# Ranking each group of four graphs by itself in the second graph layer

## What is computed

```python
x = x + gnn0(layernorm(x), adj)     # softmax(leaky_relu(s1+s2) masked by adj) @ h, then elu
x = x + ffn0(layernorm(x))          # 8 experts, the best two of each row, weighted
x = x + gnn1(layernorm(x), adj)     # the same attention with other slopes, then relu
x = x + ffn1(layernorm(x))          # 32 experts of width 32
# ffn1:
logits = xf @ router_w.T + router_b
idx = argmax(logits)                # one expert for each of the 16384 rows
h = relu(xf @ W1[idx] + b1[idx])
out = relu(h @ W2[idx] + b2[idx])
```

## Time and profile before

| | us |
|---|---|
| median of 3 executions | 1198.93 (1197.79 to 1203.39) |
| profiled execution, its own time | 1197.08 |
| its span | 1195.3 |
| PE busy over the span | 948.1 (79%) |
| DVE busy | 791.0 (66%) |
| POOL busy | 781.6 (65%) |
| ACT busy | 708.2 (59%) |

### The profile page before, as it was taken

How to read it: one execution, slowest core, us unless ns; L and a number is a source line. 1 busy time by engine, 2 the same in 40 slices (tenths; PEclk the granted TensorE clock), 3 DMA queues, 4 the chain that set the end, 5 groups by cost and what they waited for, 6 DMA issues and landing times. The chain is left out here.

```text
span 1195.3 us, 27365 instructions
## 1 busy us (share of the span) xinstructions
PE 948.1 (79%) x6789; PEld 839.2 (70%) x6789; DVE 791.0 (66%) x3492; ACT 708.2 (59%) x2414; POOL 781.6 (65%) x989
## 2 busy tenths in 40 slices
PE   5888988887179999999994899999960667666873
PEld 4677877776079999999994688888850555544653
DVE  6688898889459999999994378888873121121221
ACT  3998898886035656555552899999930333322431
POOL 4357777777617787877776048778785366666666
PEclk9999897987579999999997999999975655666555
DMA  9133432211367777777772113232213442223210
GB/s 207 37 120 118 139 102 61 60 51 38 95 180 207 203 205 206 208 203 207 196 203 60 36 51 87 76 86 76 60 42 109 109 111 83 74 82 85 64 35 8
DMA packets 147913, 130.88 MB, mean 109 GB/s; under 512 B 26450, under 2 KB 119484, under 8 KB 147760
## 3 DMA queue, kind: packets, MB, share of 16 engines
q1 hardware_dynamic: 125456, 93.02, 30.4%
q0 software_dynamic: 18272, 34.21, 8.4%
q10 hardware_dynamic: 4032, 1.89, 0.5%
HBM read 83.28 MB, written 49.61 MB: 111 GB/s over the span
## 5 line engine op out<-in xcount | busy, mean ns | idle before, releaser
L477 POOL DMA_INDIRECT xs<-staged,dst x256 | 258.9, 1011 | 77.6 <-issue 68.5
L1067 ACT ACTIVATE hT<-bank,wt 128x128 f32<-128x128 f32 x620 | 177.2, 369 | 133.4 <-PE bank L1274 81.4
L528 POOL DMA_INDIRECT out<-oq,xq x160 | 159.9, 999 | 112.2 <-DVE oq L978 66.3
L506 POOL DMA_INDIRECT x2d<-ob,xi x155 | 163.6, 1055 | 43.3 <-issue 29.1
L1260 PE MATMUL bank<-xnT,wt 128*128 128x128 f32 x1240 | 166.9, 278 | 0.7 <-issue 0.4
L1274 PE MATMUL bank<-w2s,hT 128*128 x1240 | 165.5, 276 | 0.7 <-DVE ob L951 0.5
L978 DVE SCALAR_TENSOR_TENSOR oq<-bank,xq 128x512 f32<-128x512 f32 x40 | 27.7, 692 | 197.1 <-remote 103.2
L1260 PEld LDWEIGHTS bank<-xnT,wt 128*128 128x128 f32 x1240 | 152.6, 194 | 3.1 <-issue 2.5
L1274 PEld LDWEIGHTS bank<-w2s,hT 128*128 128x128 f32 x1240 | 150.9, 192 | 1.8 <-issue 1.2
L1101 ACT ACTIVATE xnqT<-bank 128x512 f32<-128x512 f32 x40 | 23.9, 596 | 164.0 <-remote 71.0
L1016 ACT ACTIVATE p<-bank,nm 128x128 f32<-128x128 f32 x256 | 103.1, 403 | 19.1 <-DVE nm L699 13.9
(11 more groups left out here) (202 smaller groups left out, 2313.9 us busy)
## 6 DMA issues: line engine op xcount, KB each, us to landing
wt<-wpd SPq DMA_DIRECT2D x155, 258.0 KB
xq<-xs SPq DMA_DIRECT2D x160, 66.0 KB
xi<-xs SPq DMA_DIRECT2D x155, 66.0 KB
xb<-x2d SPq DMA_DIRECT2D x32, 258.0 KB
xb<-in_x SPq DMA_DIRECT2D x32, 256.0 KB
wpd<-w1c SPq DMA_DIRECT2D x56, 129.0 KB
xs<-staged,dst POOLq DMA_INDIRECT x256
out<-oq,xq POOLq DMA_INDIRECT x160
```

The source lines that it names most:

```text
L477: pool.indirect_dma_start(out=xs[l], out_offset=bass.IndirectOffsetOnAxis(ap=dst[b % ND][:, c:c + 1], axis=0), in_=stag[s][:, q, 0:ROW], i ...
L506: pool.indirect_dma_start(out=x2d, out_offset=bass.IndirectOffsetOnAxis(ap=xi[t % NXI][:, ID:ID + 1].bitcast(U32), axis=0), in_=ob[:, t % ...
L528: pool.indirect_dma_start(out=orow, out_offset=bass.IndirectOffsetOnAxis(ap=xq[j % NXQ][:, q, ID:ID + 1].bitcast(U32), axis=0), in_=oq[j % ...
L1067: last = act.activation(hT[t % 2][:, j, :], HID[t % 2][:, j, :], ACT.Gelu, bias=wt[t % NW][:, c:c + 1])
```

## The change

In layer 1 the table now holds 32 batches of one group in place of 16 batches of two; layer 0 keeps its pairs.

```diff
-BATCH = [[(2 * b, 2) for b in range(NG // 2)] for l in range(2)]
+BATCH = [[(2 * b, 2) for b in range(NG // 2)], [(g, 1) for g in range(NG)]]
```

## The result

The changed kernel took 1206.16 us (median of 11 executions, 1203.84 to 1209.66), the kernel before 1200.61 us (11, 1197.79 to 1204.42): ratio 1.0046, 95% interval 1.0034 to 1.0059. It is slower by 5.5 us (interval 4.1 to 7.1), where +3.8 was forecast. The profiled execution took 1206.29 us with a span of 1204.5, 9.2 us over that of before.

The account below looks back on a forecast made before the run. The prediction took layer 1's odd steps to be a latency loop through `route1` and `nm`; 0.15 + 7.92 - 0.53 + 0.64 - 5.07 + 0.7 = +3.8 us gave 1202.7 us, own range 1199.5 to 1206, 8 in 10 range 1196 to 1207.5.

Parts of the forecast that it names:

- Two of the signs that I had named for being wrong: Layer 1: a step under 7.0 or over 7.25 us; quick fills not beginning 2.4 us behind the last scatter.
- first rival: Layer 1 steps: the narrow loop is shorter and POOL's own work sets the pace, 1189.6 us; chance 0.07.
- the second (6.81 stays): Layer 1 steps: the pace stays at 6.81 us because slack before `pm` hides something counted, 1194.0 us; chance 0.10.
- The price of a narrow operation: DVE, layer 1: a linked operation of 128 columns takes 0.31 us, 0.01 either way, so a step is 7.14 us.
- fourth rival: PE's rank product before every transpose of `staged` adds a wait above 0.1 us per step, over +6 us; chance 0.12.
- The start of the fills: End of layer 1: last power +8.2 us, with a shorter chain behind it, so fills begin +6.1 us later, at 909.7.
- The tail, -5.07: POOL, end of layer 1: six groups of scatters in place of seven, each leaving a step sooner, saves 5.07 us.
- fixed time behind the last scatter: End of layer 1: fills crawl while scatters are under way, quick ones begin 2.4 us behind the last scatter.
- third rival: End of layer 1: fills take as long as before whatever POOL does, the late `filli` decides, 1205.0 us; chance 0.13.
- Pace: Layer 1, steps 8 to 31: 24 steps of 7.14 us in place of 6.81, +7.92 us.
- start: Layer 1, steps 6 and 7: a narrow `route1` added in step 6 moves the first `pm` of step 8 by +0.15 us.
- fills: End of layer 1: 1.4 fewer fills done in the crawl come after it at 0.52 us each, +0.7 us.

Follow-up runs that it names:

- e1: Changed kernel with `places` moved behind `scores` in layer 1 (second `oh` buffer); ratio 1.0018 to the kernel before.
- e2: Changed kernel with `scores` (`nmax`, `nm`) put ahead of `route1` in layer 1; ratio 1.0021 to the kernel before.
- e10: Changed kernel with one more, repeated linked operation of 128 columns in `route1` of layer 1; ratio 1.0172 to the kernel before.
- e6: Changed kernel, unaltered, run again on another occasion; 1149.93 us, ratio 1.0077 to the kernel before.
- e4: Changed kernel, but in layer 1 SP and ACT wait for all scatters before issuing the fills; ratio 1.0149 to the kernel before.
- e12: Changed kernel with layer 1's fills issued only after all scatters, run on a further occasion; ratio 1.0154 to the kernel before.
- e3: Changed kernel, but each group of layer 1 leaves one step later on POOL, as before; ratio 1.0075 to the kernel before.
- e11: Changed kernel with each group of layer 1 leaving one step later on POOL, run on a further occasion; ratio 1.0093 to the kernel before.
- e9: Kernel before with 15 pairs and two single groups in layer 1, the last power ahead of one group's scatters; ratio 1.0003 to the kernel before.
- e5: Kernel before, with pairs, but in layer 1 DVE does the scores ahead of `route1`; ratio 0.9993 to the kernel before.
- e8: Kernel before, with pairs, but POOL does the last three powers of layer 1 ahead of the scatters; ratio 0.9988 to the kernel before.

## Why the prediction was right in the main, and where it was off

The direction and the size held: +5.5 us was measured for +3.8, and the ratio of 1.0046 lies inside the 0.5% that had a chance of 0.67. The time of 1206.16 lies inside the range for 8 in 10 (1196 to 1207.5) but just over my forecast's own range (1199.5 to 1206). 1.7 us of the miss in time is the median of before, 1200.61 in 11 executions for 1198.93 in three. Two of the signs that I had named for being wrong did show: the mean step is 7.31 us with an ordinary one of 7.25, and the quick fills began 2.1 us behind the last scatter and not 2.4.

**What bounds a step: right.** Singles removed the alternation, each step is the loop of latencies from `pm` to `pm`, ACT and POOL wait as told. e1 and e2 take a part out of the loop, and the step falls until DVE is full; e10 puts one in, and it grows by just that part. The first rival (POOL's pace) and the second (6.81 stays) are excluded by the 7.25.

**The price of a narrow operation: too low.** "I take 0.31 and give it 0.01 either way." The seven links of a step (five in `route1`, two in `places`; I had counted nine) take about 0.325 us each; `route1` is 1.83 in place of 1.76 and `places` 0.92 in place of 0.88. A step is 7.25, just over the 7.23 that I had allowed: +2.6 us in 24 steps. The 0.31 was the interval from `lgb` to its waiter, the one narrow row that I used. It is still 0.31 in the changed kernel (792.34 to 792.65), but `lgb` is the quick one: it lasts 0.28, the others of this width 0.29. The wide ones (0.457 for a duration of 0.42, so 0.037 between end and start) and the 0.29 of `pm`, which has the same width, would have given 0.29 + 0.037 = 0.327. The Trainium skill's 75 ns per instruction (Vector Engine (DVE) Microarchitecture Reference, 5.2 Measured stream behaviour on trn2) was still further off for linked operations, as the prediction assumed.

**A term that I didn't have: PE's clock.** Singles leave PE idle for about 1 us in every step where before it was nearly full (114.28 of 120 us, now 104.98). In one step of this profile the clock was low, for 1.24 us. Together with 2.6 this explains 3.9 of the 4.1 us by which the 24 steps missed. The drop belongs to the execution and not to the kernel alone: e6 has none in these steps. By its size (12.01 / 24 = 0.50 us more in each step in place of 0.33) the pace is the fourth rival's, above 0.1 us over mine, but not by its mechanism: no wait for the rank product showed.

**The start of the fills: too early.** I had put it 6.1 us later, at 909.7; it was 914.05, 10.4 later, or 11.4 counted from the first `nm` of the layer. 4.2 of the 5.3 us between are the pace and the start; the rest was not taken apart. By the account above it cost nothing here, since the last scatter decided.

**The tail, -5.07 and the fixed time behind the last scatter: held at this level, not at the other.** In the pair of profiles the tail is -4.56 (forecast -4.96), and the first `xnq` follows the last scatter by 14.2 to 15.6 us in all four kernels profiled at the 1200 us level, although their fills start 8.4 to 15.9 us ahead of it. At the 1141 us level this time runs from 7.0 to 12.7 us (e4 and e12 apart, whose fills wait), and the profiles of e3 and e11 put the sooner leave at 0.5 to 1.6 us there. So at that level the start of the fills counts, which the change delays by more than 10 us, and the third rival's idea comes nearer. The change's price points the same way, ratio 1.0077 there (8.6 us) against 1.0046 (5.5 us), but the two intervals overlap. At the 1200 us level e9 shows that a sooner start of the fills gains nothing; e3 wasn't measured there, so that the -5.07 is real is argued from the profiles, not shown by undoing it. That the forecast was made from, and measured at, the level where its rule for the tail holds is luck: the prediction did not know of the other.

**The sum.** Pace +4.1, start +0.1, tail +0.4, fills -1.0, end -0.03 make the +3.8 into the +7.4 us of the layer. The medians differ by 5.5. The 1.8 us between the two is within what the two profiled executions differ from their medians (0.1 and 3.5 us); it was not taken apart further.

## What to carry to other kernels

Splitting a batch halves the width of its operations but not their price: from 256 to 128 columns a linked operation went from 0.457 to 0.325 us. Ask first which steps had slack: here pairs put the two chains in different steps, one of which hid its chain under another engine's work, and singles paid both in each step. Take the interval of linked operations as duration plus the gap seen between linked ones of any width, and multiply by the number of links times steps; about 0.015 us for each became 2.6. Before a term rests on how a tail ends, look for what else could end it, and whether that holds in another execution.

## What the runs showed of the hardware

The same program has two levels on different occasions, 1141 to 1143 and 1199 to 1203 us, and the chip that gave 1141 us for e5 to e8 gave 1202 us for e9 and e10; no comparison here crosses them except where said. The pace of graph layer 1 is equal at both (changed kernel: 7.25 us a step), so the difference lies elsewhere. Of the 55.0 us between the changed kernel's span and that of e6, the same kernel, 9.1 lie ahead of the layer's first `nm`, 3.0 from there to the first `xnq`, and 42.9 in mixture 1. Of the 3.0 the step with the low clock has 1.1, and the stretch behind the last scatter the other 2.0. The second level shows itself in SP's 16 fills: 8.94 us (e6) against 15.72 (changed). In such a crawl not only the transfers are slow: the view of line 316 in the kernel before has SP's register moves from 905 to 919 us at a median of 686 ns, and those from 919.5 to 924 us at 29. The views by line from 940 to 1130 us, for the kernel before at the 1200 us level and then for e6:

```profile
L528 POOL DMA_INDIRECT out<-oq,xq x119 | 119.2, 1002 | 94.3 <-DVE oq L978 59.7 <-issue 34.5
L1304 PE MATMUL bank<-xnqT,vq 128*32 128x128 f32 x250 | 54.6, 392 | 39.6 <-issue 39.6
```

```profile
L528 POOL DMA_INDIRECT out<-oq,xq x146 | 145.6, 997 | 45.7 <-issue 43.0 <-DVE oq L978 2.7
...
L1304 PE MATMUL bank<-xnqT,vq 128*32 128x128 f32 x289 | 50.4, 332 | 0.0
```

At the slower level PE sits idle for 39.6 us before its products of line 1304 with nothing to wait for ("issue"), and POOL writes 119 outputs where at the other level it writes 146. Why an occasion has one level or the other is open. It also unsettles my reading of the crawl: scatters under way are not enough for it (e6), and whether they are needed was not measured.

The other surprise is PE's clock: in an otherwise busy stretch with an idle time of 1.0 to 1.3 us in each step it fell to 0.50 (the 1.2 GHz level) for about 3 us, in one step of the changed kernel's profile and in about every fourth of e10's, and was 1.00 in the steps around. What picks these steps is open: e10's idle times don't differ between them, and e6, e3, e4, e11 and e12 have the idle time of 1.3 us without the drop. Both profiles with drops are from the 1200 us level and the five without from the other; two against five profiles don't show that the level is the reason. In e10 the mean granted clock from 700 to 890 us was 0.95, against 0.99 in the changed kernel.
